# Stage joining the first layer: tiles in pairs, one table change for both, two products on GpSimd, no loop

## What is computed

```
y   = output of the scan + D_skip * x
out = (y * sigmoid(10 * (y - max(v_th, 0.1))) * silu(z)) @ W_out
s   = out - xn                                # xn: the normalised input
g   = silu((xq @ kq) * scale_per_token + bias)   # xq, kq: rounded to 8-bit floats
x1  = x + s * g
```

## Time and profile before

| in the profiled execution | |
|---|---|
| span | 4055.7 us |
| stage `ssm_output`, first DMA issue to DVE's last instruction | 991.46 to 1171.80 us |
| busy from 1010 to 1160 us: ACT, DVE, PE, POOL | 137.35, 125.54, 89.42, 0.00 of 150.00 us |
| mean of one: table load, exp or ln, open_, half a spike, one copy of four | 1283, 1057, 1040, 706, 461 ns |
| mean of one: ysp or zsp, a, g1, gden, s, g, sg, x1 | 1218, 1225, 692, 427, 1217, 685, 1219, 1225 ns |

### The profile page before, as it was taken

The page is one execution under the profiler, slowest core; times in us unless marked ns, Lnnn a source line. Parts: engine busy times, 40 slices in busy tenths (PEclk is TensorE's granted clock), DMA queues, the critical chain, the costliest instruction groups (busy, mean ns, idle before and its releaser), DMA issues. The chain is left out here.

```text
span 4055.7 us, 64760 instructions
## 1 busy us (share of the span) xinstructions
PE 3421.6 (84%) x19475; PEld 2015.0 (50%) x19476; DVE 3205.1 (79%) x4243; ACT 2410.3 (59%) x4320; POOL 1304.2 (32%) x905
## 2 busy tenths in 40 slices
PE   8968989987559799897999999999999964389950
PEld 3445555554448689795333333333333322189950
DVE  8959999998876466467899999999999923378768
ACT  6768888885964433210577777777777750133323
POOL 4439989986014444301000000000000006644520
PEclk9979999998889899997799999999999986699975
DMA  6664444444859733395122323232232124223258
GB/s 213 251 210 168 162 157 160 163 158 148 278 180 251 201 89 92 91 291 143 26 53 61 68 55 73 53 72 57 57 71 52 31 70 126 83 81 91 89 168 294
DMA packets 531451, 521.08 MB, mean 128 GB/s; under 512 B 84784, under 2 KB 441264, under 8 KB 531040
## 3 DMA queue, kind: packets, MB, share of 16 engines
q1 hardware_dynamic: 517248, 480.45, 40.3%
q0 software_dynamic: 13952, 37.74, 2.7%
HBM read 301.15 MB, written 215.71 MB: 127 GB/s over the span
## 5 line engine op out<-in xcount | busy, mean ns | idle before, releaser
L2315 DVE TENSOR_REDUCE at_top<-at_psM 128x1 f32<-128x1024 f32 x1024 | 1205.6, 1219 | 101.2 <-PE at_psM L2174 99.8
L2283 ACT ACTIVATE at_probs<-at_psS 128x512 f32<-128x512 f32 x2048 | 1061.0, 603 | 286.3 <-PE at_psS L2200 286.3
L2200 PE MATMUL at_psS<-at_q,at_k 64*128 64x512 f32 x2048 | 803.6, 471 | 8.2 <-ACT at_probs L2283 8.2
L2174 PE MATMUL at_psM<-at_k,at_q 62*128 62x512 f32 x2048 | 705.2, 454 | 41.4 <-DMA at_vraw<-scratch_vf 21.9
L575 POOL TENSOR_TENSOR sc_prod<-sc_state,sc_c_row 128x1024 f32<-128x1024 f32 x256 | 648.7, 2564 | 84.7 <-DVE sc_state L726 72.6
L2174 PEld LDWEIGHTS at_psM<-at_k,at_q 62*128 62x128 f32 x2048 | 312.9, 190 | 621.6 <-DVE at_top L2315 539.6
L726 DVE TENSOR_TENSOR_SCAN sc_state<-sc_dec,sc_psI 128x1024 f32<-128x1024 f32 x256 | 574.3, 2276 | 43.7 <-PE sc_psI L647 34.0
L2213 PE MATMUL at_psV<-at_probs,at_v 128*32 128x512 f32 x4096 | 546.3, 605 | 0.0
L658 PE MATMUL sc_psY<-sc_prod,sc_ident 128*128 128x512 f32 x1024 | 480.4, 599 | 15.3 <-DVE sc_y L712 15.3
L2200 PEld LDWEIGHTS at_psS<-at_q,at_k 64*128 64x128 f32 x2048 | 337.7, 184 | 170.3 <-ACT at_probs L2283 160.5
L2141 POOL COPY at_v<-at_vraw 128x256 f32<-128x256 f32 x32 | 12.8, 401 | 1250.4 <-DMA at_vraw<-scratch_vf 1167.5
(11 more groups left out here) (398 smaller groups left out, 4928.7 us busy)
## 6 DMA issues: line engine op xcount, KB each, us to landing
sc_c_row<-scratch_bc SPq DMA_DIRECT2D x128, 512.0 KB, 3.7
scratch_xs<-at_zeros SPq DMA_DIRECT2D x140, 264.0 KB, 4.7
sc_b_row<-scratch_bc SPq DMA_DIRECT2D x32, 512.0 KB, 5.0
ec_y<-scratch_ys SPq DMA_DIRECT2D x32, 512.0 KB, 6.1
ex_x<-scratch_xs SPq DMA_DIRECT2D x39, 264.0 KB, 2.8
si_x<-in_x SPq DMA_DIRECT2D x16, 512.0 KB, 4.4
scratch_xn<-si_xn SPq DMA_DIRECT2D x16, 512.0 KB, 5.1
scratch_x_t<-si_xT SPq DMA_DIRECT2D x16, 512.0 KB, 5.7
```

The source lines that it names most:

```text
L2174: ins = pe.matmul(psM[t % 2][:, half * TILE:(half + 1) * TILE], rows_of(q4[j], h, 0, MAXROW)[:, c * P:(c + 1) * P], rows_of(k4[j], h, 0, M ...
L2200: pe.matmul(psS[v % 3][:], rows_of(k4[j], h, 0, GROUP)[:, c * P:(c + 1) * P], rows_of(q4[j], h, 0, GROUP)[:, half * TILE:(half + 1) * TILE ...
L2283: act.activation(probs[:, slot(j, v), :], psS[v % 3][:], ACT.Exp).then_inc(act_done, 1)
L2315: dve.tensor_reduce(top[j % 2][:, h, c:c + 1], psM[t % 2][:], AX.X, ALU.max, negate=True).then_inc(maxed, 1)
```

## The change

`ssm_output` is written anew. The loop is gone: all 16 tiles stand as straight code, in eight pairs.

- ACT does for a pair: the tanhs of the next pair, one table load that is asked for by name (`preload_act_table_set`), exp of both tiles, copies of one tile of the next pair, ln of both, copies of the other tile, exp of both. The load back to the set with tanh comes by itself before the next tanh.
- `a` and `x1` are made by POOL with `tensor_tensor` (`gated`, `joined`). The factor 1/4 of `a` goes into the weights: `wq` = wout / 4, made once by POOL, and psO = a by wq.
- DVE keeps seven instructions a tile, in an order by pairs.
- PE makes psO of both tiles of a pair, then psG of both tiles of the next.
- g1 has four buffers, all other tiles between engines two.
- SP issues the loads of y, z, xq of tiles 0 and 1 ahead of the seven of the weights; x and xn have semaphores of their own, and xn is loaded as soon as s is made.

The diff, cut:

```diff
-        two, SETS = range(2), 4
+        two, SETS, PAIRS = range(2), 4, NT // 2
...
-        ysp, zsp = m.sb("ysp", [P, H, TILE]), m.sb("zsp", [P, H, TILE])
...
+        g1 = [m.sb(f"g1_{k}", [P, SUB, D], BF16) for k in range(SETS)]
...
             def _(sp):
...
+                load_yz(0)
+                load_yz(1)
                 sp.dma_start(wout[:], halves(A["w_out"])).then_inc(weights, 16)
...
+                for j in range(PAIRS):
+                    for i in pair(j - 1):
+                        store(i)
+                        if i + 2 < NT:
+                            load_x(i + 2)
+                    for i in pair(j + 1):
+                        if i + SETS < NT:
+                            sp.wait_ge(a_ready, i + 1)
+                            sp.wait_ge(g_psum, i + 1)
+                            m.settle(sp)
+                            load_yz(i + SETS)
+                    for i in pair(j):
+                        if i + 2 < NT:
+                            sp.wait_ge(s_ready, i + 1)
+                            m.settle(sp)
+                            load_xn(i + 2)
...
+                for j in range(PAIRS):
+                    p, q = pair(j)
+                    for i in pair(j + 1):
+                        spikes(i)
+                    act.preload_act_table_set("natural_log_exp_and_others")
+                    exponential(p)
+                    exponential(q)
+                    if j + 1 < PAIRS:
+                        product(p + 2)
+                    logarithm(p)
+                    logarithm(q)
+                    if j + 1 < PAIRS:
+                        product(q + 2)
+                    reciprocal(p)
+                    reciprocal(q)
+
+            @block.gpsimd
+            def _(pool):
+                pool.wait_ge(weights, 112)
+                pool.tensor_scalar(wq[:], wout[:], 0.25, None, ALU.mult).then_inc(wq_ready, 1)
+
+                def gated(i):
+                    pool.wait_ge(ysp_ready, i + 1)
+                    pool.wait_ge(zsp_ready, i + 1)
+                    later(pool, o_psum, i - 1)
+                    pool.tensor_tensor(a[i % 2][:], ysp[i % 2][:], zsp[i % 2][:], ALU.mult).then_inc(a_ready, 1)
+
+                def joined(i):
+                    pool.wait_ge(sg_ready, i + 1)
+                    pool.wait_ge(x_loaded[i % 2], 16 * (i // 2 + 1))
+                    later(pool, x1_st[i % 2], 16 * (i // 2))
+                    pool.tensor_tensor(x1[i % 2][:], sg[i % 2][:], x[i % 2][:], ALU.add).then_inc(x1_ready, 1)
+
+                for i in pair(0):
+                    gated(i)
+                for j in range(PAIRS + 1):
+                    for i in pair(j - 1):
+                        joined(i)
+                    for i in pair(j + 1):
+                        gated(i)
...
+                pe.wait_ge(wq_ready, 1)
+                for j in range(PAIRS):
+                    for i in pair(j):
+                        out(i)
+                    for i in pair(j + 1):
+                        gate(i)
...
-                    dve.scalar_tensor_tensor(a[par][:], ysp[:], 0.25, zsp[:], ALU.mult, ALU.mult).then_inc(a_ready, 1)
...
-                    dve.tensor_tensor(x1[par][:], sg[:], x[par][:], ALU.add).then_inc(x1_ready, 1)
...
+                for j in range(PAIRS):
+                    p, q = pair(j)
+                    more = j + 1 < PAIRS
+                    for i in pair(j - 1):
+                        silu(i)
+                        weighted(i)
+                    if more:
+                        spiked(p + 2)
+                        opened(p + 2)
+                        spiked(q + 2)
+                    denominator(p)
+                    if more:
+                        opened(q + 2)
+                    denominator(q)
+                    if more:
+                        biased(p + 2)
+                    residual(p)
+                    residual(q)
+                    if more:
+                        biased(q + 2)
```

More of the change, by code:

```diff
@@ L773, in rows, with later, pair @@
             return A[name].rearrange("(i s p) d -> i p s d", p=P, s=SUB)[i, :, :, :]
-        def turns(eng, step):
-            for i in range(SETS):
-                step(i, i)
-            with eng.Fori(1, NT // SETS - 1) as turn:
-                for k in range(SETS):
-                    step(turn * SETS + k, k)
-            for i in range(NT - SETS, NT):
-                step(i, i % SETS)
-        def known(i):
-            return isinstance(i, int)
-        def yz_at(i, k):
-            return (i - k) * (48 // SETS) + 48
+        def later(eng, sem, value):
+            if value > 0:
+                eng.wait_ge(sem, value)
+        def pair(j):
+            return [i for i in (2 * j, 2 * j + 1) if 0 <= i < NT]
         with nc.Block() as block:
@@ L827, in _ @@
-                load_yz(0, 0)
-                load_yz(1, 1)
-                load_x(0, 0)
-                load_x(1, 1)
-                load_yz(2, 2)
-                load_yz(3, 3)
-                turns(sp, step)
-                store(NT - 1, (NT - 1) % 2)
+                load_yz(2)
+                load_yz(3)
+                for i in two:
+                    load_xn(i)
+                    load_x(i)
+                for i in two:
+                    sp.wait_ge(a_ready, i + 1)
+                    sp.wait_ge(g_psum, i + 1)
+                    m.settle(sp)
+                    load_yz(i + SETS)
@@ L835, in _ @@
+                for i in pair(PAIRS - 1):
+                    store(i)
                 for k in two:
@@ L865, in step, with logarithm, reciprocal @@
+                def logarithm(i):
                     act.wait_ge(gden_ready, i + 1)
-                    act.activation(glog[:], gden[:], ACT.Ln).then_inc(glog_ready, 1)
+                    later(act, grec_ready, i - 1)
+                    act.activation(glog[i % 2][:], gden[i % 2][:], ACT.Ln).then_inc(glog_ready, 1)
+                def reciprocal(i):
                     act.wait_ge(glog_ready, i + 1)
-                    if not known(i) or i >= 2:
-                        act.wait_ge(g_ready, i - 1)
@@ L870, in step @@
-                    act.activation(grec[k % 2][:], glog[:], ACT.Exp, scale=-1.0).then_inc(grec_ready, 1)
-                    if not known(i) or i + 2 < NT:
-                        spikes(i + 2, (k + 2) % SETS)
-                    if not known(i) or i + 1 < NT:
-                        product(i + 1, (k + 1) % SETS)
-                spikes(0, 0)
-                spikes(1, 1)
-                act.wait_ge(tok_ready, 1)
-                product(0, 0)
-                turns(act, step)
+                    later(act, g_ready, i - 1)
@@ new lines, in biased, with denominator @@
+                def biased(i):
+                    dve.wait_ge(g0_ready, SUB * i + SUB)
+                    later(dve, g_ready, i - SETS + 1)
+                    later(dve, gs_ready, i - SETS + 1)
+                    dve.tensor_tensor(g1[i % SETS][:], g0[i % 2][:], over_chunks(bias[:]), ALU.add).then_inc(g1_ready, 1)
+                def denominator(i):
+                    dve.wait_ge(gs_ready, i + 1)
+                    later(dve, glog_ready, i - 1)
+                    dve.tensor_scalar(gden[i % 2][:], gs[i % 2][:], 1.0, None, ALU.add).then_inc(gden_ready, 1)
@@ L993, in _ @@
-                front(0, 0)
-                turns(dve, step)
-                opened(NT - 1, (NT - 1) % 2)
-                joined(NT - 1, (NT - 1) % 2)
+                    later(dve, x1_ready, i - 1)
+                    dve.tensor_tensor(sg[i % 2][:], s[i % 2][:], g[i % 2][:], ALU.mult).then_inc(sg_ready, 1)
+                for i in pair(0):
+                    spiked(i)
+                    opened(i)
+                for i in pair(0):
+                    biased(i)
+                for j in range(PAIRS):
[18 more added lines that the diff above has]
+                        biased(q + 2)
```

167 lines of the change are left out of this document (68 added, 99 removed).

## The result

The changed kernel takes 4037.14 us (median of 15 runs, 4034.9 to 4040.18) where the kernel before takes 4026.43 on the same chip (4023.13 to 4031.09); the ratio is 1.0026, 95% interval 1.0018 to 1.0033. That is 10.7 us more (7 to 13), where 7.1 were forecast. In the profiled execution (span 4038.1 us) the stage takes 189.5 us from its first DMA issue to the end of its last x1, in place of 180.35, so 9.2 of the 10.7 us lie in this stage by the two profiles, and the rest is less than the interval. The whole spans of the two profiled executions say nothing of the change: before's is the longer one (4055.7 us), because in that execution the `er_` instructions of `experts`, from their first to the first of `ex_`, took 240.6 us and in this one 211.2, far behind the stage that was changed.

What follows compares the result with a forecast made beforehand. ACT was taken to bound the stage before the change, busy 137.35 of 150 us. Stage +2.0, late weights +4.6 and wq +0.5 made 7.1 us on 4025.9, so 4033 us, range 4014 to 4040.

Steps and rivals of the forecast that it cites:

- ACT's saving: ACT in ssm_output: two table loads a pair instead of four, gaining 4.2 to 4.7 us if ACT stayed the bound.
- The exclusion: POOL products and DVE instructions with two SBUF operands, or SBUF-to-SBUF TENSOR_SCALARs, take turns: 1.09 us on DVE, 2.20 on POOL.
- the four named: DVE instructions that POOL's a and x1 stop in each pair: second sg, next pair's first zsp, gden and g1.
- The steady pair: Mid-stage pair of tiles: DVE's 12.5 us plus four turns with POOL make 21.0 us, 0.7 more than two periods before.
- The whole stage: From ACT's first instruction to the stage's end: 169.8 us against 167.75, +2.0 us.
- The start: Prelude before ACT's first instruction: weights' DMAs behind tiles +4.6 us, POOL's wq holding DVE's TENSOR_SCALARs +0.5.
- the small vectors about 1, the landing 0.5: Last steps of the start's landing estimate: after tiles and weights' bytes, these us bring the last weights DMA in at 1002.9.
- The third rival: At the start, weights land later than their bytes say: 10.3 us instead of 4.6, whole 4039 us; chance 0.08.
- The sum: Whole kernel: 2.0 + 4.6 + 0.5 = 7.1 us more, giving 4033 us.
- The sign: Whole kernel against no change: same 0.47, slower (above 4034) 0.35, faster (below 4018) 0.18.
- The rivals without exclusion, or with some forms free: In the stage, POOL and DVE don't hinder each other (3994 us, 0.08), or only some forms are stopped (4013 to 4017, 0.14).
- the first rival: In the stage, POOL and DVE don't hinder each other: ACT bounds a pair at 15.7 us, whole 3994; chance 0.08.

Runs made afterwards that it cites:

- e8: e9 with gden made within ACT's ln by a bias of 1, leaving out its rounding to bfloat16: 3999.00 us, ratio 0.9932.
- e1: The changed kernel with a and x1 made by DVE again, wq still on POOL: 4011.23 us, ratio 0.9969.
- e6: The changed kernel with a alone made by DVE again, x1 still on POOL: 4025.17 us, ratio 0.9999.
- e7: The changed kernel with x1 alone made by DVE again, a still on POOL: 4022.50 us, ratio 0.9993.
- e5: The changed kernel with POOL's product for a replaced by four fills that read nothing: pair 16.8 us, stage 141.47 us, whole time not read.
- e9: The changed kernel with a and x1 on DVE, weights issued first, factor 0.25 back in a's product and no wq: 4004.33 us, ratio 0.9949.

## Why the prediction came out as it did

- **ACT's saving**: right. A pair needs 15.7 to 16.2 us of ACT; e8's first pairs show it, at 15.8. The load is 1.28 us and the next activation starts 1.29 behind it (1078.08 to 1079.37 and 1083.85 to 1085.14 in the changed kernel), as in the trace of before. The 2.66 us that the Trainium skill (ScalarE: Activation LUTs, "What ACT_TABLE_LOAD costs") gives for a switch are seen in neither.
- **The exclusion**: right, also for the forms that no row of before had shown. scalar_tensor_tensor (zsp, 3.38), the bfloat16 product (g1, 2.83), the bfloat16 TENSOR_SCALAR (gden, 2.56) and the 32-bit product (sg, 3.28) are all stopped. The rule of the Trainium skill (SBUF — State Buffer, "Who interferes with whom") holds in each. Those stopped are the four named, in the order named; s never is.
- **The steady pair**: 21.0 forecast, 20.9 measured. A stop costs 2.05 to 2.16 us, where 2.20 - 0.05 was taken. For e1, e6, e7 and e5 17.6, 19.3, 19.3 and 16.6 to 17.2 were expected, by placing one instruction behind another, and 17.7, 19.4, 19.2 and 16.8 were measured.
- **The whole stage**: 169.8 forecast, 169.0 measured, +1.25 in place of +2.0. ACT waits 4.4 us a pair for gden (some 5 forecast), and the copies of tile 2 start 16.95 us behind ACT's first instruction (1029.80) in place of 17.7, since the two psO there took 8.8 us together and not 9.8 (the prediction's 6.1 is none of the earlier trace rows; it is the first psO of the stage before, which took 6.09 from 1009.18):

```profile
1020.14 8.76 PE L943 MATMUL so_psO<-so_wq,so_a 128*128 128x256 f32 x32 [3.93 <-POOL so_a L908]
```

- **The start**: too small. +4.6 and +0.5 were forecast, +7.2 and +0.7 measured, 2.8 us short together. The step that failed is "the small vectors about 1, the landing 0.5" in the sum by bytes. The issue of xmax was put 6.3 us behind the first and was at 6.55, and by bytes the tiles and the large weights were to be through 9.8 us behind that first issue, at 1002.2, which is where the rate falls. But from there it was 4.2 us to DVE's start and not 1.5. The trace of before showed this tail, 4.3 us (above); the prediction shortened it to 1.5 without a row. Kept at 4.3, its own sum by bytes gives +7.3. The third rival put 10.3 us on "seven small DMAs behind full queues"; its size was too large by 3, and the full queues weren't what made the tail long.
- **The sum**: 7.1 forecast, 10.7 measured. Of the 3.6 us between them 2.8 are the start's, the stage took 0.75 back, and 1.5 lie outside the stage, less than the interval (7 to 13) can tell.
- **The sign**: the forecast of 4033 lay 1 us under the line between same and slower, with 0.47 on same and 0.35 on slower, and the shortfall of the start took it across: 4037.1, or 0.26% slower. The mechanism held; which side of the line the time fell on hung on two or three microseconds. The rivals without exclusion, or with some forms free, are excluded by the changed kernel's own rows: the pair of 20.9 us, and all four kinds of stopped instruction. e5 shows what one harmless product brings, 16.8; the 15.7 of the first rival, with both harmless, no run shows.

Left open is how POOL's wq and DVE's small TENSOR_SCALARs divide 1.6 us between them: two DVE steps were 0.70 us longer beside a wq of 1.52, so DVE wasn't shut out for its whole length there.

## What to carry to other kernels

Before moving an elementwise product from VectorE to GpSimd, count what VectorE has to do beside it: if it reads two operands from SBUF then, GpSimd's 2.3 us are VectorE's too, and the move costs VectorE more (2.1) than it takes away (1.3). What is left of the change once products and order are as they were (e9: tiles in pairs with half the table loads, straight code, more buffers, PE's and DVE's new order) is worth 20.8 us; no run takes these apart. It stands at 17.7 us a pair, where DVE's list is the bound and no longer ACT's. A gain and two losses of one change had hidden each other, and only taking them apart shows it. In a stage's first DMAs, what the first computation waits for goes first, and a vector of 1 KB behind 2.6 MB of tiles lands 6.6 us behind its issue in place of 3.1.
